# First expert layer of a fused two-block transformer: rows sent to their experts' regions in DRAM and computed in tiles

## What is computed

```python
x = x + attention0(layernorm(x), ctx)     # 16 heads of 8, softmax with a temperature from a small MLP
x = x + experts0(layernorm(x))            # the layer of this change
x = x + attention1(layernorm(x), ctx)     # 8 heads of 128, windowed with dilations 1, 2, 4, 8
x = x + experts1(layernorm(x))            # 8 experts of 64, top 2

def experts0(x):                          # 8 experts, hidden 256, top 2
    xn = rms_norm(x, norm_scale)
    scores_topk, idx = top_k(xn @ w_router.T, 2)
    weights = softmax(scores_topk)
    u, gate = split(w_up[idx] @ xn)       # 128 -> 2 x 256 for each of the two experts of a row
    down = w_down[idx] @ (u * silu(gate)) # 256 -> 128
    return sum(down * weights) + x        # x is the skip inside the layer
```

## Time and profile before

| what | value |
|---|---|
| three runs | 593.57, 592.89, 593.63 us; median 593.57 |
| the profiled execution | 593.19 us, span 591.4 us |
| mean granted clock of TensorE | 0.965 |
| busy in the span | PE 528.8, PEld 412.8, DVE 398.6, ACT 285.3, POOL 143.0 us |
| DMA | 20447 packets, 10.78 MB; mean 18 GB/s |
| DMA queues | q1 (SP) 9.10 MB, q10 (ACT) 1.18 MB, instructions 0.50 MB |

### The profile page before, as it was taken

The page is one execution under the profiler, slowest core; times in us unless marked ns, Lnnn a source line. Parts: engine busy times, 40 slices in busy tenths (PEclk is TensorE's granted clock), DMA queues, the critical chain, the costliest instruction groups (busy, mean ns, idle before and its releaser), DMA issues.

```text
span 591.4 us, 12949 instructions
## 1 busy us (share of the span) xinstructions
PE 528.8 (89%) x3952; PEld 412.8 (70%) x3952; DVE 398.6 (67%) x1306; ACT 285.3 (48%) x841; POOL 143.0 (24%) x376
## 2 busy tenths in 40 slices
PE   3899999897999969899999999778999999874996
PEld 1444444485566647788888888667999999762875
DVE  4389998966488974656656556547777877727553
ACT  0588989852565624342322223125665766732221
POOL 3232222110387771000121102120123322231000
PEclk9999999999899998899999999978999999996899
DMA  5900002001000000000000000000000000000001
GB/s 118 350 30 11 12 8 61 1 1 29 4 6 3 2 2 1 1 1 0 2 1 2 0 0 0 0 2 2 1 1 1 1 0 0 0 1 1 18 19 35
DMA packets 20447, 10.78 MB, mean 18 GB/s; under 512 B 7468, under 2 KB 18998, under 8 KB 20406
## 3 DMA queue, kind: packets, MB, share of 16 engines
q1 hardware_dynamic: 17750, 9.10, 5.5%
q10 hardware_dynamic: 2656, 1.18, 0.7%
HBM read 9.09 MB, written 1.18 MB: 17 GB/s over the span
## 4 chain that ended last, share of the span: by engine, by line
PE 76%; DVE 9%; issue 5%; ACT 4%; POOL 3%; DMA 1%; SPq 1%; DVEq 0%; POOLq 0%; ACTq 0%
PE psum L1225 10%; PE psum L1374 9%; PE psum L1179 6%; PE psum L1362 5%; PE psum L1363 5%; PE psum L1364 5%; PE psum L1415 4%; PE psum L1333 4%; PE psum L1446 4%; PE psum L1406 4%; PE psum L1426 3%; PE psum L1487 2%; PE psum L1212 2%; PE psum L1316 2%; PE psum L1474 1%
## 5 line engine op out<-in xcount | busy, mean ns | idle before, releaser
L569 ACT ACTIVATE work<-psum 128x512 f32<-128x512 f32 x64 | 38.1, 597 | 76.4 <-PE psum L1364 76.4
L500 ACT ACTIVATE wa<-psum,negmax 128x120 f32<-128x120 f32 x256 | 67.8, 376 | 10.5 <-DVE negmax L811 10.4
L1031 DVE TENSOR_TENSOR work<-psum,work 128x512 f32<-128x512 f32 x64 | 44.1, 691 | 31.4 <-PE psum L1364 25.5
L1225 PE MATMUL psum<-wa 32*128 32x480 f32 x128 | 63.1, 1082 | 2.1 <-ACT wa L500 2.0
L1374 PEld LDWEIGHTS psum<-dnT,work 128*128 128x128 f32 x512 | 62.0, 191 | 2.7
L1374 PE MATMUL psum<-dnT,work 128*128 128x128 f32 x512 | 62.3, 275 | 0.0
L597 ACT ACTIVATE work<-work,d 128x120 f32<-128x120 f32 x128 | 48.7, 381 | 21.7 <-DVE d L1103 21.7
L1041 DVE SCALAR_TENSOR_TENSOR x<-psum,gate,x 128x128 f32 (+1 forms) x128 | 36.1, 344 | 33.0 <-PE psum L1374 32.9
L1362 PE MATMUL psum<-x_hi,up_hi 128*128 128x512 f32 (+1 forms) x128 | 54.6, 426 | 2.6 <-DVE work L1031 2.3
L683 POOL TENSOR_TENSOR rstd<-mv,eps 128x1 f32<-128x1 f32 x32 | 6.1, 190 | 206.2 <-DVE mv L941 206.1
L1363 PE MATMUL psum<-x_lo,up_hi 128*128 128x512 f32 (+1 forms) x128 | 51.7, 404 | 0.0
(11 more groups left out here) (231 smaller groups left out, 1139.9 us busy)
## 6 DMA issues: line engine op xcount, KB each, us to landing
x<-in_x_dram ACTq DMA_DIRECT2D x4, 256.0 KB, 5.2
work<-in_L_ffn_w_down_dram SPq DMA_DIRECT2D x1, 1024.0 KB
wa<-mscratch SPq DMA_DIRECT2D x64, 2.0 KB
out_dram<-wa SPq DMA_DIRECT2D x4, 256.0 KB, 2.3
wa<-in_ctx_dram SPq DMA_DIRECT2D x16, 60.0 KB, 1.8
work<-in_L_xattn_Wq_dram SPq DMA_DIRECT2D x1, 512.0 KB
work<-in_L_xattn_Wk_dram SPq DMA_DIRECT2D x1, 512.0 KB
work<-in_L_xattn_Wv_dram SPq DMA_DIRECT2D x1, 512.0 KB
```

Source lines behind the costliest of these rows:

```text
L500: e = nc.scalar.activation(prob[:, z, hh, :], psum[:, 3 + 2 * half + h // 4, (h % 4) * LK:(h % 4 + 1) * LK], ACT.Exp, bias=negmax[:, z, hh ...
L1031: nc.vector.tensor_tensor(hT[:, e % 2, j, :], psum[:, 2 * j, :], silu[:, j, :], ALU.mult).then_inc(c_h, 1)
L1225: m = nc.tensor.matmul(psum[:, 3 + g, 0:4 * LK], qs[rows, z, :], kexp[rows, z].rearrange("p i k -> p (i k)"), start=True, stop=True)
```

## The change

The first expert layer computes only the two chosen experts of each row. Rows are sent to regions in DRAM, one region per expert, gathered in tiles of 128 rows of one expert.

- Two parts: the first 6 sequences and the other 10. Part 0 has 19 tiles, part 1 has 27 (2 x sequences + 7, the most that 8 experts can need); tiles that stay empty are computed too.
- In stage b the normalized rows of all sequences stay in SBUF (`xrow`); the scale of the norm goes into the up weights when these are turned. The split of rows and up weights in high and low parts is gone, and so is Pool's copy of the keys. ScalarE copies each sequence's router scores to SBUF. A DRAM area of 18176 rows is filled with zeros by two DMAs of the ScalarE queue before stage b.
- VectorE chooses the experts of a part (`pick_experts`), TensorE counts with a triangular matrix how many rows before each go to the same expert (`rank`), VectorE makes of it each row's place (`place_rows`) and, on one partition, a table of each tile's expert and first row (`tile_table`). Part 0: steps 12, 13 and 17 of stage b; part 1: tiles 0 to 2 and 6.
- Pool scatters each sequence's rows twice (12 and 20 indirect DMAs of 128 rows), and later gathers each sequence's two results (2 x 16 indirect DMAs).
- SP loads each tile and stores its result over it; it and TensorE read the tile's row or expert from the table into a register.
- The tails of part 0 run beside tiles 26 and later; those of part 1, with their gathers and sums, run inside the steps of stage d: Pool does `c_tail` first in its step, VectorE last.
- Stages b, c and d are written out without loops (`peel=NB`). The bias of the u products moves into a second product with a row of ones.

The core of the diff:

```diff
+PARTS = (PART0, Part(PART0.seqs, NB - PART0.seqs, PART0.tiles, PART0.rows))
+RING_C = 4
@@ sync
+            def load_tile(n):
+                h = int(n >= PARTS[1].first_tile)
+                i = n - PARTS[h].first_tile
+                if i == 0:
+                    sp.wait_ge(k_tab, h + 1)
+                    sp.wait_ge(scattered[h], 16 * PARTS[h].slots)
+                if n >= RING_C:
+                    sp.wait_ge(ct_xt, n - RING_C + 1)
+                row = sp.value_load(tile_tab[0:1, h, 1, i:i + 1], min_val=0, max_val=ROWS - P)
+                tile_rows[n] = row
+                sp.dma_start(ct_x[:, n % RING_C, :], by_expert[bass.ds(row, P), :]).then_inc(ld_ct[n % RING_C], 16)
+            def store_tile(n):
+                sp.wait_ge(ct_ye, n + 1)
+                sp.dma_start(by_expert[bass.ds(tile_rows.pop(n), P), :], ct_y[:, n % RING_C, :]).then_inc(st_ct[n % RING_C], 16)
+            AHEAD = RING_C + 2
...
+            for n in range(TILES):
+                if n + AHEAD < TILES:
+                    load_tile(n + AHEAD)
+                store_tile(n)
@@ scalar
+            for i in range(ZERO_PARTS):
+                act.dma_start(by_expert[i * chunk:(i + 1) * chunk, :].rearrange("(p a) d -> p a d", p=P),
+                              zeros.unsqueeze(1).to_broadcast([P, chunk // P, D])).then_inc(zeroed, 16)
...
+            tile_pipeline([(1, ct_gate), (2, ct_hidden), (0, ct_halves), (0, ct_tail)])
@@ gpsimd
+            def scatter(h, i):
+                if i == 0:
+                    pool.wait_ge(k_rows, h + 1)
+                    pool.wait_ge(zeroed, 16 * ZERO_PARTS)
+                b = PARTS[h].first + i % PARTS[h].seqs
+                nc.gpsimd.indirect_dma_start(by_expert[:, :], bass.IndirectOffsetOnAxis(rows_at[:, h, i:i + 1], 0),
+                                             xrow[:, b, :], None).then_inc(scattered[h], 16)
...
-            software_pipeline(pool, [(0, b_stage), (3, tail_rstd("b")), (2, b_split), (6, tail_keep("b"))], peel=8)
+            software_pipeline(pool, [(0, b_stage), (3, tail_rstd("b")), (3, b_scatter)], peel=NB)
...
+            def c_tail(at, h):
+                if at in range(PARTS[h].seqs):
+                    gather(PARTS[h].first + at)
+                for late, stage in ((1, tail_rstd), (3, tail_keep)):
+                    if at - late in range(PARTS[h].seqs):
+                        b = PARTS[h].first + at - late
+                        stage("c")(b, b % 2)
...
-            software_pipeline(pool, [(2, d_stage), (4, tail_rstd("d")), (6, tail_keep("d"))], peel=8)
+            software_pipeline(pool, [(0, lambda b, z: c_tail(b, 1)), (2, d_stage), (4, tail_rstd("d")),
+                                     (6, tail_keep("d"))], peel=NB)
@@ vector
+            tile_pipeline([(0, lambda n: ct_turned(n) if n < TILES else None), (1, ct_product), (3, ct_result), (0, ct_route),
+                           (0, lambda n: c_tail(lambda late: c_step(n, late), 2))])
...
             software_pipeline(dve, [(5, tail_norm("d")), (1, d_scores), (0, d_queries), (2, d_weights),
-                                    (2, add_bias(1, d_xb)), (4, d_residual), (4, tail_stats("d", d_x)), (4, tail_aggr("d"))], peel=8)
+                                    (2, add_bias(1, d_xb)), (4, d_residual), (4, tail_stats("d", d_x)), (4, tail_aggr("d")),
+                                    (0, lambda b, z: c_tail(lambda late: d_step(b, late), 1))], peel=NB)
@@ tensor
+            def ct_turn(n):
...
+                tile_expert[n] = pe.value_load(tile_tab[0:1, h, 0, i:i + 1], min_val=0, max_val=NE - 1)
+                pe.wait_ge(ld_ct[n % RING_C], 16 * (n // RING_C + 1))
+                if n:
+                    pe.wait_ge(ct_xe, n)
+                turn(psum[:, 2, 0:P], ct_x[:, n % RING_C, :], P).then_inc(ct_xt, 1)
+            def ct_up_project(n):
...
+                w = upT[:, bass.ds(tile_expert[n] * UP_TILES, UP_TILES), :].rearrange("p t c -> p (t c)")
+                nc.tensor.matmul(psum[:, n % 2, :], ct_xT[:, n % 2, :], w, start=True, stop=True).then_inc(ct_up, 1)
...
+            tile_pipeline([(0, lambda n: ct_turn(n) if n < TILES else None), (1, ct_up_project), (2, ct_turn_hidden),
+                           (3, ct_down_project), (0, lambda n: rank(1) if n == RANK_TILE else None),
+                           (0, lambda n: c_part(c_logits, c_step(n, 5))),
+                           (0, lambda n: c_part(c_turn, c_step(n, 3)))])
...
-            pe.wait_ge(tails["c"]["keep"], NB)
             pe.wait_ge(halved, 2)
```

More of the change, by code:

```diff
@@ L66, in shape_constants @@
     groupmask = (part // DK0 % GROUP0 == np.arange(GROUP0)[None, :]).astype(np.float32)
+    tri = np.triu(np.ones((P, P), np.float32), 1)
+    region_rows = np.tile(np.concatenate([np.tile(part.first_row + np.arange(NE) * part.region, part.slots)
+                                          for part in PARTS]), (P, 1))
+    tile_no = np.tile(np.arange(PARTS[1].tiles), (P, 1))
+    tile_ends = np.tile(np.arange(MOST) * P, (P, 1))
+    upto = np.tile(np.tri(NE).reshape(1, -1), (P, 1))
     cols, at, parts = {}, 0, []
@@ L78, in software_pipeline @@
 def software_pipeline(eng, stages, n=NB, peel=4):
-    assert all(lag <= peel - 2 for lag, _ in stages) and (n - peel) % 2 == 0
+    assert peel == n or all(lag <= peel - 2 for lag, _ in stages) and (n - peel) % 2 == 0
     def step(b, parity):
@@ L89, in software_pipeline @@
         step(b, b % 2)
-    with eng.Fori(0, (n - peel) // 2) as i:
-        for parity in range(2):
-            step(i * 2 + (peel + parity), parity)
+    if n > peel:
+        with eng.Fori(0, (n - peel) // 2) as i:
+            for parity in range(2):
+                step(i * 2 + (peel + parity), parity)
     for b in range(n, n + peel):
@@ L458, in build, with tile_pipeline, c_step, d_step @@
         T_CLIPPED, T_SCALED, T_PARTS = 2, 3, 7
-        ROUTE_SLOT = 1
-        STATS_SLOTS, NORM_SLOTS, TURN_SLOTS, LOGITS_SLOTS = (range(a, a + SEQS) for a in (1, 2, 3, 4))
         R_DIFF, R_COUNT = 4, 13
+        ROUTE_B, ROUND_TILE, C_FIRST = PART0.seqs + 6, 4, PART0.tiles + 7
+        ZERO_PARTS = 2
+        RANK_TILE, PLACE_TILE, TABLE_TILE = 1, 2, 6
+        def tile_pipeline(stages, lag=5):
+            for n in range(TILES + lag):
+                for late, stage in stages:
+                    if 0 <= n - late < TILES or late == 0:
+                        stage(n - late)
+        def c_step(n, late):
+            b, odd = divmod(n - C_FIRST - late, 2)
+            return b if not odd and 0 <= b < PART0.seqs else None
+        def d_step(b, late):
+            at = b - 1 - late
+            return PART0.seqs + at if 0 <= at < PARTS[1].seqs else None
         @block.scalar
@@ L550, in tail_evict, with tail_scores, run @@
                 return run
-            def b_split(b, z):
-                tiles = bass.ds(b * 2, 2)
-                nc.scalar.copy(up_hi[:, tiles, :], upT[:, tiles, :]).then_inc(b_hi, 1)
+            def tail_scores(ph):
+                s, dst, done = tails[ph], *((lg, b_lk) if ph == "b" else (u1s, d_u))
+                def run(b, z):
+                    act.wait_ge(s["lg"], b + 1)
+                    nc.scalar.copy(dst[:, b, :], scored_at(ph, b)).then_inc(done, 1)
+                return run
@@ new lines, in ct_halves, with ct_tail @@
+            def ct_halves(n):
+                if n == ROUND_TILE:
+                    nc.scalar.copy(vo_hi[:, :, :], vo1[:, :, :]).then_inc(rounded, 1)
+                    act.wait_ge(ld_late, 16 * (N_LATE + 1))
+                    nc.scalar.copy(w1_hi[:, :], ew1.rearrange("p n f -> p (n f)")).then_inc(rounded, 1)
+                    nc.scalar.copy(rows_r[:, :, :], expert_rows).then_inc(rounded, 1)
+            def ct_tail(n):
+                for late, stage in ((4, tail_evict("c")), (6, tail_scores("c"))):
+                    b = c_step(n, late)
+                    if b is not None:
+                        stage(b, b % 2)
@@ L975, in done, with route @@
+            def route(logits, bias):
+                count = [0]
                 def done(ins):
@@ L1070, in _, with ct_route @@
[L1070 to L1074 removed]
+                assert count[0] == R_COUNT
+            def ct_route(n):
+                if n == 0:
+                    pick_experts(1)
+                if n == PLACE_TILE:
+                    place_rows(1)
+                if n == TABLE_TILE:
+                    tile_table(1)
@@ new lines, in _, with c_tail @@
+            c_stats, c_aggr, c_norm = tail_stats("c", c_added), tail_aggr("c"), tail_norm("c")
+            def c_tail(seq_at, norm_late):
+                for late, stages in ((norm_late, (c_norm,)), (0, (c_combine, c_stats, c_aggr))):
+                    b = seq_at(late)
+                    if b is not None:
+                        for stage in stages:
+                            stage(b, b % 2)
+            tile_pipeline([(0, lambda n: ct_turned(n) if n < TILES else None), (1, ct_product), (3, ct_result), (0, ct_route),
```

(12 more changed lines are left out.)

564 lines of the change are left out of this document (359 added, 205 removed).

## The result

The changed kernel took 597.86 us, the median of four runs (596.98 to 599.09), the kernel before beside it 593.52: ratio 1.0077 (95% interval 1.0057 to 1.0096). I had forecast 568.3 and faster. Run again unchanged in another group of runs it took **573.6 us** (e9, ratio 0.9662, 0.9646 to 0.9678), in a third 599.1 (e13, 1.0096). Within a group its executions agree to 2.1 us. The kernel before stays at 593 in all of them, and one chip showed both levels.

The account below looks back on a forecast made before the run. The prediction took the expert layer as bound by TensorE, which starves at both ends, and the second attention as TensorE with VectorE near. Sum: 593.2 - 48.9 (second attention starting earlier) + 24 (its lengthening) = 568.3 us; range 539 to 605.

Parts of the forecast that it names:

- Fill: First attention: the new zero fill beside the small mask loads, taken as 2 us.
- the two ends, 0 and 33: Bounds on the fill's cost: 0, or 33 us if the mask loads queued behind all of it.
- Scatters: Pool's indirect DMAs at 1.4 us each, between 0.42 and 2.8; first tile at 235, second part's scatters hidden.
- rival of slow Pool DMAs (609): Pool's queue before tile 0 and tile 19: indirect DMAs cost 2.8 us each, +41, 609 us; chance 0.13.
- First attention: Step 4.43 us, dropped Pool work gains 0; fill adds 2, choice, rank and places of part 0 add 3.
- Drain from the last softmax to tile 0: End of first attention: table adds 3.5, dropped high and low parts give back 1.5, +2; first tile at 235.
- Tile step: Expert layer: 2.0 us a tile, set by register read (1.0) and SP's issues; ends 1.65 and 2.8.
- The layer: First expert layer: 96 us of tile steps plus 7.3 of work put between tiles, 103.3 us.
- stretch of each row gather: Second attention: gathers beside two-input VectorE operations stretch by up to 1 us each, nothing in the sum.
- Second attention: Lengthens by +24 us (ends 0 and +35) from later sequences' tails and Pool's order before this stage's 1/sigma.
- six steps at 11.1 us: Second attention, steps 5 to 10: 11.1 us each against 7.95, VectorE waiting 2.8 for Pool; +19.
- steps 1 to 4: Second attention: TensorE's turn waits for VectorE's normalization, next scores behind it; +1 for two, +1.8 for two, 5.5.

Follow-up runs that it names:

- e9: The changed kernel run again unchanged in another group of runs; 573.6 us, ratio 0.9662 to the kernel before.
- e13: The changed kernel run unchanged once more, in a third group of runs; 599.11 us, ratio 1.0096 to the kernel before.
- e1: Changed kernel with the zero fill issued by SyncE near 101 us instead of by ScalarE at 139.7; 589.37 us.
- e3: Changed kernel with the second part's twenty scatters started eight tiles later, after tile 10 is turned and copied; 602.27 us.
- e16: Changed kernel with each scatter of the second part waiting for the landing of the one before; 606.84 us.
- e2: Changed kernel with GpSimd's second-attention step reordered: context rounding and this stage's 1/sigma before the later sequences' gather, 1/sigma and copy; 593.48 us.
- e8: Changed kernel with the second part's 20 scatters writing 32 instead of 128 elements of each row, to a separate tensor; 574.11 us.
- e4: Changed kernel without its register reads, each tile's expert and first row being constants (output not the layer's); 591.68 us.
- e14: Kernel before the change with 30 scatters added in the expert layer, to a tensor nobody reads; 615.03 us, beside 593.1 without them.
- e5: Kernel before the change with 30 scatters added in the expert layer, to a tensor nobody reads; 592.73 us, beside 593.16 without them.

## Why the prediction was wrong

*Fill: taken as 2 us, measured 9.2* (first softmax at 155.14 to 155.20, 145.95 before; without the fill, in e1, at 144.47). This step fails at either level. I had the two ends, 0 and 33, and placed the term by the mask loads alone. I bounded the data of the fill and never its issue: ScalarE's queue holds the softmaxes, and an issue there had only been seen with small transfers.

*Scatters: 1.4 us each, measured 1.27 on GpSimd. The step that failed is that I priced them on GpSimd's queue and to their landing, and nowhere else.* At the slow level 6.0 us are lost before tile 0 (5.0 of them in the drain) and 17.9 in the tiles, 24 of the 29.6 us by which I missed. The 17.9 are the scatters' by e3 and e16. That the 6.0 are too is read from where the engines stand still, beside the first part's pairs of scatters; no run changed that alone. No row of the kernel before could show it, since it has no such DMA; but "what else may wait while this runs" was a bound to draw, and my rival of slow Pool DMAs (609) stood on the wrong queue.

*First attention*: 3 us for the choice, measured 4.6 at the step before softmax 13 (199.43 to 207.98, 8.55, against 3.97 for the steps before it); but the other fourteen steps shrank to 4.04 us in the mean (quick level), which I had at 0. I had taken 4.43 for the step before from four late ones; all fifteen of the kernel before have a mean of 4.24. Drain from the last softmax to tile 0: 20.5 implied, 22.9 at the quick level.

*Tile step: 2.0 taken, 1.82 measured* in tiles 8 to 21 (e9, stores 272.18 to 295.87), register read 0.72 where I took 1.0. Once the tails run beside the tiles it is 2.11 (stores 300.02 to 325.31), where I had them hidden in 2.0. Tile 19 isn't late at the quick level. The layer there is 98.8 us against 103.3: this part was right in its cause and 4.5 us too dear. The stretch of each row gather by up to 1 us beside VectorE's work doesn't show either: all 32 take 0.94 to 1.04 us.

*Second attention: +24 forecast, +25.2 measured*, and by the cause that was named, VectorE's 2.74 us at the head of a step behind GpSimd's other 1/sigma. It wasn't confined to six steps at 11.1 us: eight took 10.66 (388.95 to 474.20). But the cause was only the first of two: the ring through TensorE's turn, which I had priced for steps 1 to 4 alone, stood behind it (nine times in e2's rows), and taking the first away alone gave back 5 of the 20 us that I then expected.

At the quick level the forecast's sum is off by 5.1 us of span: fill +7.2, rest of the first attention -1.4, drain +2.4, layer -4.5, second attention +1.3. The steps hold there but for the fill, and the small sum is in part luck, since the layer's 4.5 us too much hide half of what the fill and the drain cost. The slow level, the first one measured, needs the cost that I hadn't seen.

## What to carry to other kernels

Price a DMA on three accounts: the queue that issues it (the 18176 short rows of the fill held it for 15 us), the transfer, and everyone else while it runs; put large fills on a queue that has nothing to do for that time. When a wait is taken away, look for the ring behind it before counting the gain. A kernel with a train of GpSimd scatters should be timed in several groups of runs, since one of them says little about it.

## What the runs showed of the hardware

- Two fill DMAs of 4544 KB in 512-byte rows hold the issuing queue 15.4 us (ScalarE, changed kernel) and 15.0 us (SyncE, e1).
- An indirect DMA of 128 rows takes 0.96 us on GpSimd and 1.27 from one to the next, whether a row has 512 bytes or 128 (e8).
- A register read from SBUF costs SyncE 0.72 us (changed kernel against e4).
- A train of such scatters stops the other engines at one level (e14: 22 us for 30 of them in a layer without other transfers) and not at the other (e5: 592.73 us beside 593.16). The level holds for a whole group of runs, isn't the chip's, and what sets it is not known. At the slow level 2.5 us between scatters prevent it (e16).
